# A recommender tower on one core: thirteen instead of eleven tables read by one-hot matmuls, and a new order of steps

## What is computed

```python
e = jnp.stack([tbl_0[ids[:, 0]], ..., tbl_25[ids[:, 25]]], axis=1)      # 512 x 26 x 128
sd = jnp.einsum('bfd,bd->bf', e, dense)
ss = jnp.einsum('bfd,bgd->bfg', e, e)
z = jnp.concatenate([dense, sd, ss[:, iu, ju]], axis=1)                 # 128 + 26 + 325
h = jnp.concatenate([z, dense], axis=1)                                 # 607
h = jnp.maximum(h @ W_top1 + b_top1, 0.0)                               # 512
h = jnp.maximum(h @ W_top2 + b_top2, 0.0)                               # 256
y = h @ W_top3                                                          # 512 x 1
```

## Time and profile before

| | |
|---|---|
| median of three runs | 122.44 us (114.56 to 128.39) |
| profiled execution | 114.91 us |
| its span, first to last instruction | 112.6 us |
| TensorE busy (matmul) | 101.9 us, 90% |
| VectorE busy | 79.4 us, 70% |
| ScalarE busy | 65.9 us, 58% |
| GpSimd busy | 64.2 us, 57% |
| read from HBM | 12.18 MB |

### The profile page before, as it was taken

How to read it: one execution, slowest core, us unless ns; L and a number is a source line. 1 busy time by engine, 2 the same in 40 slices (tenths; PEclk the granted TensorE clock), 3 DMA queues, 4 the chain that set the end, 5 groups by cost and what they waited for, 6 DMA issues and landing times.

```text
span 112.6 us, 2801 instructions
## 1 busy us (share of the span) xinstructions
PE 101.9 (90%) x1092; PEld 89.6 (80%) x1092; DVE 79.4 (70%) x218; ACT 65.9 (58%) x150; POOL 64.2 (57%) x66
## 2 busy tenths in 40 slices
PE   6969999979996999998899979995999969996993
PEld 6758888858775888898799868984999949996890
DVE  4699999999999999992307880888049960786002
ACT  4657489599569385692307970888049930768120
POOL 7477777777777777777777777777771000000000
DMA  3997797658999992111111221221221000000000
GB/s 91 258 256 162 202 303 217 151 151 226 288 306 292 322 313 54 41 54 52 47 52 52 67 52 47 63 63 47 52 55 38 6 0 0 6 0 0 0 0 1
DMA packets 5030, 12.35 MB, mean 110 GB/s; under 512 B 1725, under 2 KB 1853, under 8 KB 5018
## 3 DMA queue, kind: packets, MB, share of 16 engines
q1 hardware_dynamic: 2906, 8.15, 25.4%
q0 software_dynamic: 1920, 3.94, 12.9%
q10 hardware_dynamic: 192, 0.10, 0.3%
HBM read 12.18 MB, written 0.00 MB: 108 GB/s over the span
## 4 chain that ended last, share of the span: by engine, by line
PE 58%; DVE 12%; DMA 10%; ACT 7%; POOL 5%; issue 4%; SPq 1%
PE dots L470 18%; PE dots L519 14%; DVE pairs L366 11%; PE hidden L544 8%; DMA rows<-tbl,gather_idx 7%; PE hidden L470 7%; POOL rows L264 5%; ACT pairs L303 5%; DMA table<-tbl 4%; PE turned L499 3%; PE last_layers L568 2%; PE turned L544 2%; PE dots L440 1%; ACT h L344 1%; SPq L214 1%
## 5 line engine op out<-in xcount | busy, mean ns | idle before, releaser
L264 POOL DMA_INDIRECT rows<-tbl,gather_idx x60 | 61.6, 1026 | 20.1 <-issue 16.5
L366 DVE COPY pairs<-dots 27x128 f32<-27x128 f32 (+8 forms) x88 | 23.7, 269 | 17.4 <-PE dots L519 14.8
L373 DVE TENSOR_SCALAR onehot<-ids_h 125x512 fp32r<-125x512 f16 x88 | 32.4, 426 | 1.0 <-ACT ids_h L309 1.0
L303 ACT COPY pairs<-dots 27x128 f32<-27x128 f32 (+8 forms) x88 | 21.0, 238 | 18.8 <-PE dots L519 16.8
L470 PE MATMUL dots<-onehot,high 125*128 125x512 f32 (+1 forms) x64 | 22.9, 382 | 0.0
L470 PE MATMUL dots<-onehot,low 125*128 125x512 f32 (+1 forms) x64 | 21.6, 363 | 0.0
L319 ACT CAST high<-table 125x1024 fp32r<-125x1024 f32 (+1 forms) x12 | 11.8, 982 | 11.3 <-DMA table<-tbl 5.4
L519 PEld LDWEIGHTS dots<-embT 128*64 128x64 f32 x512 | 15.5, 138 | 2.2 <-issue 2.1
L519 PE MATMUL dots<-embT 128*64 128x54 f32 x512 | 16.0, 223 | 1.3 <-DVE pairs L366 0.7
L381 DVE TENSOR_TENSOR low<-table,high 125x512 fp32r<-125x512 f32 x22 | 14.9, 678 | 0.0
L544 PE MATMUL hidden<-pairs,wp 128*128 128x128 f32 x112 | 13.4, 277 | 0.8 <-ACT pairs L303 0.8
(11 more groups left out here) (52 smaller groups left out, 101.8 us busy)
## 6 DMA issues: line engine op xcount, KB each, us to landing
table<-tbl SPq DMA_DIRECT2D x10, 448.0 KB
wp<-w_pairs SPq DMA_DIRECT2D x2, 512.0 KB
rows<-tbl,gather_idx POOLq DMA_INDIRECT x60, 2.6
table<-tbl SPq DMA_DIRECT2D x10, 52.0 KB
wd<-w_dense SPq DMA_DIRECT2D x1, 512.0 KB
w2s<-w SPq DMA_DIRECT2D x1, 512.0 KB
table<-tbl SPq DMA_DIRECT2D x2, 224.0 KB
denseT<-dense_t SPq DMA_DIRECT2D x1, 256.0 KB, 4.1
```

The costliest lines, as they stand in the source:

```text
L264: pool.indirect_dma_start(out=rows[:, t % 2, n, :], out_offset=None, in_=tables[GATHERED_TABLES[n]][:, :], in_offset=bass.IndirectOffsetOn ...
L303: return nc.scalar.copy(dst, src)
L366: return nc.vector.tensor_copy(dst, src)
L373: nc.vector.tensor_scalar(onehot[:, i % STAGES, c, :], ids_h[:, i % ID_BUFFERS, :], float(c), None, ALU.is_equal).then_inc(onehot_ready, 1)
```

## The change

Tables 2 and 8, of 1250 rows, join the one-hot tables: thirteen tables, of which the fourth and the seventh in the new order have 10 chunks of 125 rows. The four buffers that held tables of one size (`table`, `high`, `low`, `onehot`) become three each, sized by the largest table that comes into them. There are three buffers of ids instead of four, and `y` is put into a part of `wd` that is free by then. Thirteen tables per tile are gathered, 52 gathers, in batches of 4, 4, 4 and 1. The list of steps is new: both late halves stand behind D0; W14 is gone; P1 moves behind layer 1 of tile 0; D2 and D3 stand ahead of Y0 and Y1; the relu and the result copy of layers 2 and 3 are steps of their own (H, V). The id spread for table 3 stands behind table 0 instead of ahead of it. Gathers number 43 and up wait for D0, 49 and up for D1; the other holds are gone. Batches alternate between the PSUM banks `turned` and `last_layers`, the last one uses a bank of the dots.

```diff
-ONEHOT_TABLES = [0, 3, 4, 5, 7, 11, 15, 17, 18, 19, 21]
-ONEHOT_ROWS = 1000
+ONEHOT_TABLES = [0, 3, 4, 2, 5, 7, 8, 11, 15, 17, 18, 19, 21]
+ONEHOT_ROWS = [1250 if f in (2, 8, 10, 22, 23, 24, 25) else 1000 for f in ONEHOT_TABLES]
...
+CHUNKS = [rows // ROW_PARTS for rows in ONEHOT_ROWS]
...
-ID_BUFFERS = 4
+STAGE_CHUNKS = [max(CHUNKS[s::STAGES]) for s in range(STAGES)]
+ID_BUFFERS = 3
...
-    HELD_BY_DOTS, HELD_BY_BATCH, HELD_BY_LAYER1 = {40: 1, 51: 2}, {46: 10, 48: 11, 53: 12}, {55: 1, 57: 2}
+    HELD_BY_DOTS = {43: 1, 49: 2}
...
-            T0 T1 B0.0 T2 B0.1 T3 B0.2 T4 B0.3 T5 B1.0 T6 T7 B1.1 T8 B1.2 T9.0 B1.3 T9.1 T9.2
-            T10.0 B2.0 T9.3 T9.4 D0 C0.0 T10.1 T10.2 T10.3 T10.4 C0.1 P0 B2.1 P1 W14 B2.2
-            D1 C1.0 B2.3 L0.0 L0.1 R0 C1.1 B3.0 M0 Y0
-            D2 C2.0 B3.1 L1.0 L1.1 R1 C2.1 P2 B3.2 M1 B3.3 Y1
-            D3 C3.0 L2.0 L2.1 R2 C3.1 P3 M2
-            L3.0 Y2 L3.1 R3 M3 Y3""".split()]
-
-        PLACERS = [0, 0, 0, 0, 0, 0, 0, 0, 1, 0, 1, 0, 1, 0, 1, 1]
-
-        APART = 2 * BATCHES + 2
-        BESIDE = (1, 3, 5)
+            T0 T1 B0.0 T2 B0.1 T3 T4 B0.2 T5 B0.3 T6 B1.0 T7 B1.1 T8 B1.2 T9 B1.3 T10 B2.0 T11.0 T12.0 B2.1
+            D0 C0.0 T11.1 T11.2 T11.3 T11.4 A11 T12.1 T12.2 T12.3 T12.4 C0.1 P0 B2.2 B2.3 A12
+            D1 C1.0 L0.0 L0.1 R0 C1.1 P1 B3.0 M0 H0
+            D2 Y0 C2.0 V0 B3.1 L1.0 L1.1 R1 C2.1 P2 B3.2 M1 H1 B3.3
+            D3 Y1 C3.0 V1 L2.0 L2.1 R2 C3.1 P3 M2 H2
+            L3.0 Y2 V2 L3.1 R3 M3 H3 Y3 V3""".split()]
+
+        PLACERS = [0, 0, 0, 0, 0, 0, 0, 0, 0, 1, 0, 1, 1, 1, 0, 1]
...
+        BATCH_BANKS = "TLTLTLTLTLTLTTTD"
...
-                    if t + IDS_AHEAD < N_ONEHOT:
+                    if 0 < t < N_ONEHOT - IDS_AHEAD:
                         spread_ids(t + IDS_AHEAD)
...
                     last.then_inc(table_selected, 1)
+                    if t == 0:
+                        spread_ids(IDS_AHEAD)
```

More of the change, by code:

```diff
@@ L89, in dlrm_tower @@
         zeros = sb("zeros", [128, 128], F16)
[L90 to L93, removed]
+        table = [sb(f"table{i}", [ROW_PARTS, n, DIM]) for i, n in enumerate(STAGE_CHUNKS)]
+        high = [sb(f"high{i}", [ROW_PARTS, n, DIM], F32R) for i, n in enumerate(STAGE_CHUNKS)]
+        low = [sb(f"low{i}", [ROW_PARTS, n, DIM], F32R) for i, n in enumerate(STAGE_CHUNKS)]
+        onehot = [sb(f"onehot{i}", [ROW_PARTS, n, BATCH], F32R) for i, n in enumerate(STAGE_CHUNKS)]
         denseT = sb("denseT", [128, BATCH])
@@ L171, in lows_to @@
         def lows_to(i, chunk):
-            return 2 * i + 1 + chunk // HALF
+            return 2 * i + 1 + chunk // half(i)
         def loads_of(i):
@@ L211, in load_rows @@
             def load_rows(i, first, last, done):
-                rows_of_part = tables[ONEHOT_TABLES[i]][:, :].rearrange("(p c) d -> p c d", c=ROW_CHUNKS)
+                rows_of_part = tables[ONEHOT_TABLES[i]][:, :].rearrange("(p c) d -> p c d", c=CHUNKS[i])
                 for a, b in ROW_PIECES:
-                    sp.dma_start(table[a:b, i % TABLE_BUFFERS, first:last, :], rows_of_part[a:b, first:last, :]
+                    sp.dma_start(table[i % TABLE_BUFFERS][a:b, first:last, :], rows_of_part[a:b, first:last, :]
                                  ).then_inc(done, 16)
@@ L318, in split_high @@
                         act.wait_ge(table_selected, i - STAGES + 1)
-                    nc.scalar.copy(high[:, i % STAGES, first:last, :], table[:, i % TABLE_BUFFERS, first:last, :]
+                    nc.scalar.copy(high[i % STAGES][:, first:last, :], table[i % TABLE_BUFFERS][:, first:last, :]
                                    ).then_inc(high_ready, 1)
@@ L330, in step @@
                     nc.scalar.copy(embT[:, samples, t], selected[t % STAGES][:, samples]).then_inc(table_placed, 1)
-                elif kind == "table" and i == 4:
+                elif kind == "late half":
                     act.wait_ge(table_selected, t + 1 + len(late))
@@ L380, in split_low @@
                     dve.wait_ge(table_selected, i - STAGES + 1)
-                nc.vector.tensor_tensor(low[:, i % STAGES, first:last, :], table[:, i % TABLE_BUFFERS, first:last, :],
-                                        high[:, i % STAGES, first:last, :].bitcast(F32), ALU.subtract
+                nc.vector.tensor_tensor(low[i % STAGES][:, first:last, :], table[i % TABLE_BUFFERS][:, first:last, :],
+                                        high[i % STAGES][:, first:last, :].bitcast(F32), ALU.subtract
                                         ).then_inc(low_ready, 1)
@@ L421, in _ @@
             for n in range(2):
[L422 removed]
+                make_onehot(0, half(0) * n, half(0) * (n + 1))
                 split_low(0, n)
@@ L448, in step @@
             def step(kind, t, i=0):
-                if kind == "warming":
-                    pe.wait_ge(table_placed, N_ONEHOT + 1)
-                    warm(t)
-                elif kind == "table" and i == 0:
-                    if t + IDS_AHEAD < N_ONEHOT:
+                if kind == "table" and i == 0:
+                    if 0 < t < N_ONEHOT - IDS_AHEAD:
                         spread_ids(t + IDS_AHEAD)
@@ L457, in step @@
                     samples = slice(0, HALF_BATCH if t in late else BATCH)
-                    for first, after in ((0, HALF), (HALF, ROW_CHUNKS)):
+                    for first, after in ((0, half(t)), (half(t), CHUNKS[t])):
                         order = [(part, c) for c in range(first, after) for part in (high, low)]
```

102 lines of the change are left out of this document (54 added, 48 removed).

## The result

The changed kernel takes 119.75 us, the median of four runs (119.39, 119.74, 119.76 and one of 135.94). The kernel before, measured beside it, took 114.56, 115.09, 122.44 and 128.39. In their ordinary course, which three of the four runs of the one and two of the other show, the ratio is 1.042 with an interval of 1.035 to 1.049: the change makes the kernel slower by 4%. The plain medians of four, 119.75 and 118.77, are only 0.8% apart, because half of the runs before are long ones. Every ratio from here on is the time over that of the kernel before beside it, in ordinary executions, with its interval behind it.

What follows compares the result with a forecast made beforehand. VectorE, nearly level with TensorE and gathers, bounds the kernel up to tile 0's dots. From 114.91 us: +5.1 there, -0.4, -1.35, +0.35 behind, with roundings 118.7; plus 0.8 gives 119.5 us, range 115.8 to 126.3.

Steps and rivals of the forecast that it cites:

- the sum: Whole kernel, from the profiled 114.91 us: later first dots +5.1, tail steps giving some back; span 116.4, execution 118.7 us.
- the 0.8 between 118.7 and 119.5: Whole execution: 0.8 us added for what is left of the run-to-run excess over the profiled execution.
- B: TensorE falls to its lower clock around the first dots: up to 3.9 us longer, 123.4 us; chance 0.10.
- The tail: Steps behind the first dots, reordered: said to give back 1.3 us against the 5.1 lost at the first dots.
- One sign: Stretch before the first dots: TensorE would show no wait for gathers.
- One sum: VectorE's last one-hot, before the first dots: moves from 49.75 to 59.6 us, or 59.3 with splits no dearer.
- From the profiled execution to the median: Late gathers, four batches by 2 us, would make the old median's extra 7.5 us; with 5 us slack, change avoids them.
- rival A: Spread unrelated to gathers; whatever lengthens runs hits both kernels alike: +3.3%, 126.2 us against the median shown; chance 0.37.
- the last sign on record: Across runs: if the changed kernel's spread as widely as before, gathers weren't the reason and rival A holds.
- C: Up to the first dots VectorE's work is cheaper and TensorE's own sum decides: 58.4 us, execution 116.4; chance 0.08.
- TensorE alone would be at D0 at 58.4: Up to tile 0's dots: TensorE's 51.6 us of work from 6.8 on, earlier than VectorE allows (60.7).
- The holds cost nothing: Last gathers, held for the first two tiles' dots: even at the longest landing, 4.8 us, 10 us of slack remains.

Runs made afterwards that it cites:

- the guard: Changed kernel with VectorE waiting, from table 4 on, for the gather batch due then: 118.83 to 119.68 us, and 129.23 and 129.42; ratio 1.048.

## Why the prediction was wrong

**Where it was right: the sum.** VectorE without idle to 59.6 us: 59.63. D0 at 60.7, released by ScalarE's placement: 61.04, and released by it. D0 to D1 10.65: 10.72. D1's end to D2 7.2: 83.20 - 75.70 = 7.50. D2's end to D3 9.2: 9.29. D3's end to L3.0 7.65: 7.82. The sum's 118.7 us stands against 119.04 in this profile and 119.39 to 119.76 in the first runs; the 119.5 on record is within 0.25 us of the median of 119.75. That closeness is partly luck: the 0.8 between 118.7 and 119.5 comes from no row, and the median holds one long execution. TensorE's clock stays at 1.00, so B is out. The tail gives 0.85 instead of 1.4: each of its three steps came out 0.1 to 0.3 us longer, the one from D1's end to D2 most. One sign failed without weight: TensorE did wait for a gather before D0, 0.80 us at 20.26. One sum has a slip without weight: with splits no dearer for 640 elements a period would be 3.93 + 0.70 = 4.63 us and VectorE's end 49.75 + 2 x 4.63 = 59.0, not 59.3. The split of 640 elements measured 0.73 to 0.74 us, near the 0.75 that was taken.

**Where it failed: "From the profiled execution to the median".** The step says that the spread comes from gathers that land 2 us late four times over, that the changed kernel has 5 us of slack at each, and that "its runs stay near the sum". From it I compared 119.5 with 122.44 and called it faster. Three things in it are wrong. A gather was rightly suspected, but not its size: in the changed kernel it is one gather held for 24 us (16 with the guard), not four late by 2. The slack of 5 us can't cover that, and so the changed kernel's runs did not stay near the sum: 8 of 16 were long, 15 to 17 us above the fastest beside them, where the kernel before had long ones of 8 and 14 us in its first runs and of 6 to 17, and once of 140, on the sixth chip. And the median of 122.44 came from three runs of which two were long; the fourth run alone moves it to 118.77. The forecast should have set 118.7 against the profiled 114.91, which the text had done one paragraph before and then left. The 7.5 us that were to fall on the kernel before alone had no run behind them.

**What came is rival A's result**, slower by 3.3% in the sum and 4.2% measured. Its condition, that D0's loss exceeds what the tail gives back, is met: 5.44 against 0.85, or 4.6 us where the sum had 3.8. On the second and fifth chips the ratio is higher (1.065 and 1.054). Part of it is that the kernel before is faster there: 111.7 us of span instead of 112.6 for the one with two pauses, with D0 at 55.11; on the second chip the changed kernel is slower besides, with two of three ordinary runs at 121.7 to 121.8. But A's reason, that the spread has nothing to do with gathers, was not it. So the last sign on record misled: the changed kernel's runs spread as widely as before, which was to clear the gathers, and yet a gather was the reason.

**C could not have come in full.** "TensorE alone would be at D0 at 58.4" left out ScalarE's placement behind the last matmul (0.6 and two handovers), took table 0 at full pace though VectorE paces it (6.13 to 10.77, 4.64 instead of 3.65), and had no wait for gathers, where 0.80 stood at 20.26. With 1.87 us less of VectorE D0 was at 60.23 and could not have been much earlier, since TensorE no longer paused.

**"The holds cost nothing", and gain nothing:** true where D0 takes 3.96 us beside gathers, as the rows of the one profile showed. On the fourth chip the holds are worth 9 us; on the third, which has no run with the same kernel and the holds, that isn't known. On both the changed kernel with pauses beats the old one by 4%. Whether it does so without pauses is open: it wasn't run there unedited. That the old kernel is slow there for the same reason is argued, not shown.

The Trainium skill ("SBUF — State Buffer", section "SBUF: two separate sides") describes a port that VectorE and GpSimd share as an exclusive lock, and a trap in which GpSimd can't write the descriptors of its DMAs while VectorE runs certain instructions, copies among them. The traces agree as to who waits for whom (23.98 us, 16.21 and 2.61, each ended 0.82 to 0.83 us behind VectorE's stop); that the port is the reason no run here shows. By the Trainium skill the lock lasts for one instruction; here the gather stayed out over some sixty of them. The prediction had weighed only transfers that share the DMA engines, which bears on landings of 4.97 us instead of 2.41 and not on a gather of 24.

## What to carry to other kernels

Compare a sum made from one profiled execution with that execution, never with a median from elsewhere: what lies between the two is a finding of its own, and has to be explained before it is claimed as a gain. Where one engine runs without a single gap, look whether one instruction of another engine beside it lasts far longer than its fellows; here a pause of 0.14 us ended such a one, and the new order of the tail alone gained nothing. Work that moves from gathers to an engine that is already full moves that engine's end by all of it (9.88 us here) and the first dots by what stood idle or movable between the two (5.44 us).

## What the runs showed of the hardware that was not expected

A GpSimd gather, 0.94 us with VectorE idle and mostly 0.94 to 1.7 beside it, can last 24 us while VectorE's instructions follow one another. In the changed kernel 8 of 16 executions were long, and the two of them that were profiled had such a gather. It was issued at 24.3 to 24.8 us, around VectorE's first split of table 4, and always right behind one of 1.65 to 1.70 us; as another one issued there passed in 0.99 us, why these are held is open. A gap of 0.14 us ended it in two profiles of the changed kernel, and one of 0.17 us in one of the kernel before; three shorter holds ended behind a one-hot of 8 columns with no gap at all.

The same program differs by chip: the kernel before took 112 to 116 us in its ordinary course on three, 136 to 155 on two others. Profiles of the changed kernel from those two show TensorE's dots breaking off with nothing to wait for, in the one without holds as long as gathers are issued; the kernel before was not profiled there.

After TensorE had been idle for 14.80 us its matmuls of 512 columns started 0.43 us apart from 55.5 to 58.5 us, at a granted clock of 0.51, which is the 1.2 GHz level, and 0.227 apart from then on, at a granted clock of 1.00.
